# Gate weight rows of the expert mixtures: broadcast through a DRAM scratch instead of a TensorE product

## The reference

```
# L0_ffn (after an attention part), used twice; D_FF = 128, one shared expert beside the eight
rw = softmax(xf @ Wr.T + expert_bias)
topw, topi = top_k(rw, 2);  topw = softmax(topw)
combine = sum(one_hot(topi, 8) * topw[..., None], axis=1)          # [token, expert]
shared = (silu(xf @ sW1.T) * (xf @ sW3.T)) @ sW2.T
h = silu(einsum('td,efd->etf', xf, eW1)) * einsum('td,efd->etf', xf, eW3)
eo = einsum('etf,edf->etd', h, eW2)
out = X + shared + einsum('te,etd->td', combine, eo)

# L1_ffn, used twice; H = 256, no shared expert
top_logits, sel = top_k(xt @ w_gate, 2);  probs = softmax(top_logits)
h = silu(xt @ w1[e]) * (xt @ w3[e]);  y[e] = h @ w2[e]
out[t] = sum over the two chosen e of probs * y[e, t]
```

## Time and profile before

| | us |
|---|---|
| median of 3 runs | 2752.49 (2752.12 to 2756.4) |
| span of the profiled execution | 2757.4 |

### The profile page before, as it was taken

One profiled execution on the slowest core, in us unless ns is written; L12 is line 12 of the kernel. 1 busy time (PEld: TensorE's weight loads), 2 busy tenths in 40 slices (PEclk: granted clock), 3 DMA queues, 4 the chain that ended last, 5 costly groups with the idle time before them and its releaser, 6 DMA issues. The chain is left out here.

```text
span 2757.4 us, 40750 instructions
## 1 busy us (share of the span) xinstructions
PE 2492.9 (90%) x12972; PEld 1587.4 (58%) x12972; DVE 1977.2 (72%) x4522; ACT 1522.7 (55%) x2424; POOL 1484.2 (54%) x1371
## 2 busy tenths in 40 slices
PE   4477998998789989989999899998999999979999
PEld 3344565666756566644444478776444444357877
DVE  6865776775667667756666588887777778668887
ACT  4632454444435544446666456654677677656665
POOL 5924654443265544356666555654766566335554
PEclk8787899998969999989999999999999999889999
DMA  1001110000021000010000100000000000010000
GB/s 47 0 3 29 36 34 25 1 1 19 1 49 39 13 26 1 1 56 1 1 1 1 45 1 1 1 1 16 1 1 1 1 0 1 1 43 9 8 5 12
DMA packets 38561, 36.73 MB, mean 13 GB/s; under 512 B 12888, under 2 KB 28120, under 8 KB 38104
## 3 DMA queue, kind: packets, MB, share of 16 engines
q1 hardware_dynamic: 38360, 34.26, 4.6%
HBM read 19.42 MB, written 2.10 MB: 8 GB/s over the span
## 5 line engine op out<-in xcount | busy, mean ns | idle before, releaser
L2328 DVE TENSOR_REDUCE l_diffneg_max<-psum 128x1 fp32r<-128x512 f32 x512 | 335.7, 685 | 96.6 <-PE psum L2066 92.3
L4475 POOL TENSOR_TENSOR l_moe1sc<-l_moe1s,l_moe1bcs 128x512 f32<-128x512 f32 x192 | 266.3, 1394 | 235.8 <-ACT l_moe1s L4284 197.7
L2243 ACT ACTIVATE l_diffweights<-psum 128x1024 f32<-128x1024 f32 x256 | 261.9, 1025 | 138.3 <-PE psum L2095 137.4
L2066 PE MATMUL psum<-l_diffkz,l_diffQ 128*128 128x512 f32 (+1 forms) x512 | 238.3, 484 | 2.9 <-DVE l_diffneg_max L2328 2.0
L4373 DVE TENSOR_TENSOR x<-l_moe1sc,psum 128x512 f32<-128x512 f32 x256 | 174.4, 681 | 92.8 <-POOL l_moe1sc L4475 82.0
L2868 ACT ACTIVATE l_lightswapped<-psum 32x512 f32<-32x512 f32 x304 | 179.0, 589 | 100.8 <-DVE l_lightturned L2960 97.4
L4380 DVE TENSOR_TENSOR l_moe1g_lo<-x,l_moe1g_hi 128x512 fp32r<-128x512 f32 x256 | 224.5, 878 | 1.1 <-ACT l_moe1g_hi L4263 1.1
L4284 ACT ACTIVATE l_moe1s<-psum 128x512 f32<-128x512 f32 x256 | 153.3, 600 | 100.8 <-PE psum L852 93.7
L1592 DVE TENSOR_REDUCE l_attn0neg_max<-psum 128x1 fp32r<-128x512 f32 x256 | 167.3, 683 | 54.5 <-PE psum L1326 51.8
L173 POOL TENSOR_TENSOR settled<-powers 128x1 f32<-128x1 f32 x111 | 35.2, 317 | 305.9 <-DVE l_alibimv L699 73.5
L1498 ACT ACTIVATE l_attn0weights<-psum 128x1024 f32<-128x1024 f32 x128 | 130.2, 1023 | 121.7 <-PE psum L1348 121.7
(11 more groups left out here) (603 smaller groups left out, 7096.0 us busy)
## 6 DMA issues: line engine op xcount, KB each, us to landing
l_attn0Q<-l_attn0q_hi SPq DMA_DIRECT2D x128, 64.0 KB, 2.0
l_moe1w_raw<-in_moe_w SPq DMA_DIRECT2D x20, 256.0 KB, 5.5
l_attn0Q<-l_attn0q_lo SPq DMA_DIRECT2D x64, 64.0 KB, 2.0
l_moe0w_raw<-in_moe_w SPq DMA_DIRECT2D x20, 128.0 KB, 2.5
x<-in_x SPq DMA_DIRECT2D x8, 256.0 KB, 4.9
out<-x SPq DMA_DIRECT2D x8, 256.0 KB, 2.3
open_raw<-in_moe_w SPq DMA_DIRECT2D x8, 128.0 KB
l_attn0Q<-l_attn0max_rows SPq DMA_DIRECT2D x64, 2.0 KB, 1.7
```

Of the source, the lines that this page charges most:

```text
L2066: nc.tensor.matmul(ps[:, bank, :], Q[rows, n % 4, st * P:(st + 1) * P], kz[rows, n % 4, hh, :], start=True, stop=True).then_inc(pe_max.sem ...
L2243: nc.scalar.activation(weights[:, tt, 2 * pair:2 * pair + 2, :], ps[:, S[m % 2]:S[m % 2] + 2, :], ACT.Exp, scale=SCALE).then_inc(act_exp.s ...
L2328: nc.vector.tensor_reduce(neg_max[:, n % 2, st, row:row + 1], ps[:, bank_of(("max", n, b)), :], AXX, ALU.max, negate=True).then_inc(vec_ma ...
L4475: nc.gpsimd.tensor_tensor(sc[:, n % 2, h, :], s[:, n % 2, h, :], bcs[:, n % 2, :], ALU.mult).then_inc(pool_sc.sem, pool_sc.step("sc", h))
```

## The change

The fp32r hi and lo rows, `rows_low`, the second copy of `comb`, the matrix `pick` and `weight_rows` on PE and ACT are gone, and so is bank BC. ACT copies the turned weights once, in fp32, to `open_rows` (`rows_out`). SP stores rows 0 to 7 of it (16 KB) to a DRAM scratch `gate_rows[j]`, waits for the store, and loads pairs of rows back, each pair (4 KB, contiguous) to all 128 partitions: 512 KB a transfer, four a sequence. `bcs` grows from two rows to a ring of six. `scale_slot` on DVE and POOL waits for the pair's DMA. In moe0 AT_COMB moves from 8 to 7. In the layers before a mixture SP stores sequence 0's rows and waits for that before the block ends.

```diff
-        inc(v.tensor_tensor(self.comb[:, :, 0:8], ...), "comb", 0)
-        inc(v.tensor_tensor(self.comb[:, :, LO_ROW:LO_ROW + 8], ...), "comb", 1)
-    def rows_low(self, d, j, bank):
...
+        inc(v.tensor_tensor(self.comb[:, :, 0:8], ...), "comb")
+    def store_rows(self, sp, j):
+        sp.wait_ge(self.act_comb.sem, self.act_comb.done(j, "rows"))
+        sp.dma_start(self.core.dram["gate_rows"][j], self.core.open_rows[0:8, :]).then_inc(self.rows_stored, 16)
...
-    def rows_high(self, a, j, bank):
+    def rows_out(self, a, j, bank):
+        if j > self.begins:
+            a.wait_ge(self.rows_stored, 16 * (j - self.begins))
         a.wait_ge(self.pe_comb.sem, self.pe_comb.done(j, "comb"))
-        self.core.nc.scalar.activation(self.rows(j), ...)
+        self.core.nc.scalar.activation(self.core.open_rows[:, :], ...)
...
-    AT_CHOICE, AT_E2, AT_WEIGHTS, AT_COMB = (4, 4, 5, 8) if moe.shared else (2, 2, 3, 5)
+    AT_CHOICE, AT_E2, AT_WEIGHTS, AT_COMB = (4, 4, 5, 7) if moe.shared else (2, 2, 3, 5)
+    ROWS = 6
-        bcs = sb("bcs", [P, 2, T])
+        bcs = sb("bcs", [P, ROWS, T])
...
+            def spread_rows(j, experts):
+                for e in experts[::2]:
+                    k = rowed(j * NE + moe.shared + e)
+                    if k >= ROWS:
+                        (waits for the scaling of rows k - ROWS and k - ROWS + 1)
+                    two = core.dram["gate_rows"][j, e:e + 2, :] ... .to_broadcast([P, 2 * T])
+                    sp.dma_start(bcs[:, k % ROWS:k % ROWS + 2, :] ..., two).then_inc(row_loaded[k % ROWS // 2], 16)
...
-            weights_in.sync_part(sp)
+            for g in range(weights_in.groups):
+                spread_rows(0, range(2 * g, min(2 * g + 2, ROWS)))
+                weights_in.sync_group(sp, g)
             if opening:
                 opening.sync_part(sp)
+            spread_rows(0, range(ROWS, moe.experts))
+            for j in range(1, NSEQ):
+                chooser.store_rows(sp, j)
+                sp.wait_ge(chooser.rows_stored, 16 * j)
+                spread_rows(j, range(moe.experts))
...
-            def weight_rows(n):          # on PE, before up(n)
-                nc.tensor.matmul(ps[:, BC, :], pick[:, e - moe.shared, :], comb_rows(j), start=True, stop=True)
-            def weight_rows(n):          # on ACT, before silu(n)
-                copy(bcs[:, n % 2, :], ps[:, BC, :])
...
             def scale_slot(n, h):
-                d.wait_ge(act_bc.sem, act_bc.done(rowed(n), "row"))
+                row_ready(d, n)
```

More of the change, by code:

```diff
@@ L257, in logits_read @@
         d.wait_ge(self.pe_gate.sem, self.pe_gate.done(j, "gate"))
-        d.wait_ge(self.vec_gate.sem, self.vec_gate.done(j, "comb", 1, back=1))
+        d.wait_ge(self.vec_gate.sem, self.vec_gate.done(j, "comb", back=1))
         if self.bias is None:
@@ L344, in __init__ @@
             comb = ctx.enter_context(core.nc.sbuf_tensor(f"l{n}_next_comb", [P, NQ, P], F32))
-            self.gate = Gate(core, ctx, f"l{n}_next", self.first.bias if layer == "moe0" else None, self.first.gate, comb,
-                             lambda j: core.open_rows[:, :])
+            self.gate = Gate(core, ctx, f"l{n}_next", self.first.bias if layer == "moe0" else None, self.first.gate, comb)
         self.counted, self.averaged = sem("statistics_vector"), sem("means_vector")
@@ L1230, in freed @@
             if what == "comb":
-                return opening.gate.vec_comb.sem, opening.gate.vec_comb.done(0, "lo")
+                return opening.gate.act_comb.sem, opening.gate.act_comb.done(0, "rows")
             if what == "max":
@@ L2408, in pair_of_sequences @@
                             opening.gate.weights(d, 0)
-                        if last and (G, m) == (7, 1):
-                            opening.gate.rows_low(d, 0, bank_of(("q", 10)))
             ident = core.ident[:, :].rearrange("p (h r) -> p h r", r=STRIP)
@@ L3066, in _ @@
             tail(NSEQ - 1)
-            opening.gate.rows_low(d, 0, EVEN)
         @block.gpsimd
@@ L4237, in _ @@
                 j, e = divmod(n, NE)
-                if EARLY <= n < N and not is_shared(n):
-                    weight_rows(n)
                 if real(n):
@@ L4268, in head_hi @@
                 copy(h_hi[:, j % 2, :], ps[:, MISC, :]).then_inc(act_hi.sem, act_hi.step("hi"))
-            def weight_rows(n):
-                act_bc.start()
-                if n >= 2:
-                    for h in range(HT):
-                        scaling_done(a, n - 2, h)
-                a.wait_ge(pe_bc.sem, pe_bc.done(rowed(n), "row"))
-                copy(bcs[:, n % 2, :], ps[:, BC, :]).then_inc(act_bc.sem, act_bc.step("row"))
             def silu(n, h):
```

123 lines of the change are left out of this document (55 added, 68 removed).

## The result

The changed kernel takes 2726.4 us (median of 4, 2721.9 to 2731.8), the kernel before beside it 2754.4 us: a ratio of 0.9895 with a 95% interval of 0.9873 to 0.9916, so 1.05% or 28 us faster. The forecast was 2711 us, 41 us faster; the time lies inside the range (2692 to 2735), near the late-rows rival (2732), but it isn't rows in moe0 that took most of what is missing.

A forecast was written before the change was run, and what follows sets the result against it. The prediction took PE's summed work inside the mixtures as the bound: 60.1 - 7.6 - 6.0 - 2.3 - 2.8 - 0.1 = 41.3 us off the 2752.5 us median gives 2711 us, range 2692 to 2735.

The forecast's parts named there:

- late-rows rival: In moe0, store and load take 7.7 us together, PE waits 1.5 us in 14 sequences: 21 us, 2732 us; chance 0.19.
- Row products: On PE in both mixture kinds, 256 products removed at 0.23 us (moe1) and 0.24 us (moe0) save 60.1 us.
- Waits in moe1: PE's one 0.40 us wait in later moe1 sequences swallows one row product of 0.23 us in each of 12: 2.8 us.
- The rival that DVE binds half of moe1: DVE's full slots hold PE in moe1, four rows of eight give nothing: 12.9 us instead of 5.1, 2719 us; chance 0.12.
- Starts: At mixture starts, row loads ahead of weight group 1 delay the first silu, giving back 7.6 us in moe0, 6.0 in moe1.
- Rows in time in moe0: In moe0 a pair arrives 6.9 us after the turning, due at 7.0; PE waits only if it takes over 7.4.
- dearer starts: Upper bound at the mixture starts: row loads hold back weight group 2 as well, double the cost, 14 us more.
- Slow broadcast: A row pair's load to all partitions takes 9.1 us, PE waits 97 us in moe0 and moe1: 2808 us; chance 0.09.
- The price by the Trainium skill: For moe0's rows, fixed 2.0 us plus bytes / 436 GB/s: store 2.0, load 3.2, pair there 6.5 us after the turning.

The follow-up runs named there:

- e7: Changed kernel with PE's down product in moe1 three slots behind the up products instead of two: 2709.3 us, ratio 0.9869 to the kernel before.
- e9: Kernel before the change with PE's down product in moe1 three slots behind the up products instead of two: 2743.5 us, ratio 0.9963.
- e1: Changed kernel without moe1's row loads after the first three, later experts reading those six rows again: 2730.9 us, ratio 0.9913 to the kernel before.
- e5: Changed kernel, but POOL's first scaling of expert 5 in moe1 waits for DVE's first g_lo of expert 3: 2718.5 us, ratio 0.9883.
- e6: Changed kernel, but DVE's first g_lo of expert 3 in moe1 waits for POOL's first scaling of expert 5: 2746.5 us, ratio 0.9988.
- e4: Changed kernel, but SP issues weight groups 0 and 1 ahead of the row loads at a mixture's start: 2717.1 us, ratio 0.9859.
- e8: Changed kernel with the weights in moe0 turned in slot 8, as before the change, instead of 7: 2748.6 us, ratio 0.9992.
- e2: Changed kernel, but DVE scales experts 1 and 6 of a moe1 sequence instead of 1 and 3: 2734.2 us, ratio 0.9930.
- e3: Kernel before the change, but DVE scales experts 1 and 6 of a moe1 sequence instead of 1 and 3: 2755.7 us, ratio 1.0001.

## Why the prediction was right or wrong

- **Row products, 60.1 us.** Right as a sum of PE's work: 1.87 us a moe0 sequence (predicted 1.9), and 1.7 us a moe1 sequence once nothing else stands in the way (e7 against e9).
- **Waits in moe1, 2.8 us for the 12 later sequences: this step failed.** It took the one wait of 0.40 us, let one row product stand in it, and counted the other seven in full. Measured is a gain of 0.03 to 0.4 us in nine of ten steady sequences where 1.6 was predicted. The rival that DVE binds half of moe1 (12.9 us instead of 5.1) had the right place and was still too mild. What both missed is that DVE's 84% and the duration of `g_lo` weren't free numbers. The two engines met before as well (`g_lo` took 878 ns on average before and 900 after), but not at this place: in the steady stretch its maximum was 1314 ns, and it is 1825 now that PE's pace brings POOL's scaling ahead. e1 excludes the transfers, e5 and e6 show the order of the two engines as a cause, and e7 that a longer lead for DVE removes the loss.
- **Starts, 13.6 us.** The mechanism was right: e4 gives back 10.9 us outside the steady sequences of its trace, 9.3 by the medians. For the first moe0 the later `silu` and PE's wait are as predicted, 4.0 and 4.04 us; in the second the `silu` is late by 3.2, and in moe1 by 1.9 and 2.6 us instead of 4.1. Yet outside the steady sequences the four blocks came out 16.7 us dearer than the removed products account for (10.1 in moe0, 6.6 in moe1), and the prediction had counted 16.4 there (7.6 and 8.8, with the waits of the moe1 sequences that lie there). So the sum came out about right with moe0 too low and moe1 too high; the 5.8 us that e4 doesn't give back aren't explained.
- **Rows in time in moe0.** Right, to 0.2 us: used 7.1 us after the turning, predicted 6.9 and due at 7.0. That it is so close is partly luck, since the errors of the store (1.46 us, counted 1.8) and of the load (4.2, counted 3.9) cancel. What I had not counted is the spread of the store, 2.7 and 3.3 us twice in 14 sequences, which cost 1.2 us. The late rows that I gave 21 us need turning a slot later (e8).
- **Slow broadcast.** Excluded: the median of a pair, from issue to landing, was 4.6 us in moe0 and 3.8 in moe1, not 7.3.
- **The price by the Trainium skill.** That rule ("Anatomy of one DMA") gave 6.5 us from the turning to the rows and the nearest rows of the trace 6.9; measured were 7.0 to 7.1. The trace's price was the nearer one. The page fits its rule on transfers that GpSimd issues, and these are SP's.
- **The range held the time by luck in part.** Its upper end stood for late rows and dearer starts. Late rows cost 1.2 us, and what filled it is the failed step in moe1.

Not settled is why e2 and e3 lengthen a sequence by 1.0 to 1.1 us (in e2 either kind, 36.9 to 38.0 and 38.07 to 39.2): that the waits moved to other slots is seen, which pair of instructions meets there isn't shown.

## What to carry to other kernels

When an instruction leaves an engine that is 98% busy, look at the engine that is 84% busy and ask what its durations will be at the new pace, not only how often it was waited for at the old one. A wait of 0.4 us in every round marks a chain that is only that far behind: it keeps what the next remedy gives, until its consumer stands a slot further back. A transfer that is free in the middle of a block isn't so at its start, where everybody waits for the first weights: put it behind them.

## What the runs showed of the hardware

- Two instructions of DVE and POOL that start within 20 ns of each other decide, by which of them is held up, over 1.13 us, and a program then has two lengths per round (36.9 and 38.07 us) with nothing else different. A part of the scatter between executions can come from such ties.
- A larger part comes from elsewhere: the layer diff took 535.6 us in the profile of e4, at a granted clock of 0.93 and with PE busy for 511.3 us, and 515.3 us in that of e9, at 0.98 and 491.6 us, with the same 2820 matmuls. The profiles of e6 and e9 are the shortest executions of their runs (2731.4 us of a median of 2746.5, 2730.3 of 2743.5) and have the two shortest diff layers.
- Even a tiny instruction is hit: L308, 128 x 4 elements on DVE, takes 164 ns in moe0, where POOL scales nothing, and 1248 ns in moe1, beside POOL's scaling (and 4.53 us in attn0, at 425.78 us, beside a sum of POOL's that takes 4.56 us):

```profile
L308 DVE TENSOR_SCALAR l_moe0den<-l_moe0e x6: 164/164/164, 501.3 to 618.9; 128x4 f32<-128x4 f32 x6
...
L308 DVE TENSOR_SCALAR l_moe1den<-l_moe1e x6: 1002/1248/1253, 1625.6 to 1815.7; 128x4 f32<-128x4 f32 x6
```

- Reading 4 KB of DRAM into all 128 partitions (512 KB) takes 3.8 to 4.6 us from issue to landing (medians in moe1 and moe0), no more than loads of 512 KB of different bytes in the same trace (4.2 and 4.5 us, and one of 8.2). The 16 KB store ahead of it takes 1.46 us until SP goes on, and 2.7 and 3.3 in two of moe0's 14.
